# Local attention on one core: each pair's scores as two 64-row matmuls over three score banks, the value projection in the queries' bank, the output product one pair earlier, the queries' square behind ScalarE's copies

## The reference, cut to what matters

```
# per batch and layer: n = 2048 tokens, 8 heads of 64, windows of 128 tokens
q, k, v = split(shift_token(x) @ wqkv)             # 256 -> 3 x 512
q = l2norm(q) * q_scale;  k = l2norm(k) * k_scale
q, k = rotary_xpos(q, k)
# each window of 128 queries looks at its own 128 keys and the 128 before them
sim  = einsum('bhwid,bhwjd->bhwij', 8 * q, k2)     # 128 x 256 for a head and window
attn = softmax(where(mask, -big, sim))
x = x + einsum('bhwij,bhwjd->bhwid', attn, v2) @ wo
```

## Time and profile before

| | |
|---|---|
| median of 3 runs | 4049.13 us (4045.39 to 4050.89) |
| profiled execution | 4053.28 us, its span 4051.5 us |
| PE busy | 3685.3 us, 91% of the span |
| PEld, DVE, ACT, POOL busy | 44%, 69%, 51%, 22% |
| the four local attention stages, first transpose to last add | 1193.0 to 1479.2, 1619.0 to 1903.3, 3197.2 to 3483.1, 3622.6 to 3908.1 |

### The profile page before, as it was taken

How to read it: one execution, slowest core, us unless ns; L and a number is a source line. 1 busy time by engine, 2 the same in 40 slices (tenths; PEclk the granted TensorE clock), 3 DMA queues, 4 the chain that set the end, 5 groups by cost and what they waited for, 6 DMA issues and landing times. The chain is left out here.

```text
span 4051.5 us, 59853 instructions
## 1 busy us (share of the span) xinstructions
PE 3685.3 (91%) x19604; PEld 1769.1 (44%) x19604; DVE 2796.6 (69%) x7007; ACT 2072.7 (51%) x3717; POOL 895.6 (22%) x801
## 2 busy tenths in 40 slices
PE   7999977999979989998979999689999799899988
PEld 5333334333335555555543333343333455555555
DVE  2998866998856643665349987769987666436644
ACT  3366643466656641565125667334667566316641
POOL 2001015001024322332220010150010333213322
PEclk8899988899989999999989999889999899999999
DMA  4222002222020010100032220022220200110000
GB/s 94 38 33 33 1 3 52 36 33 33 1 66 6 1 54 6 28 1 6 21 75 33 33 33 2 2 56 32 33 33 1 66 6 1 54 28 6 1 11 26
DMA packets 129571, 109.04 MB, mean 27 GB/s; under 512 B 40884, under 2 KB 122332, under 8 KB 128220
## 3 DMA queue, kind: packets, MB, share of 16 engines
q1 hardware_dynamic: 129256, 105.12, 12.9%
HBM read 41.15 MB, written 4.19 MB: 11 GB/s over the span
## 5 line engine op out<-in xcount | busy, mean ns | idle before, releaser
L737 ACT ACTIVATE probs<-banks 128x1024 f32<-128x1024 f32 (+3 forms) x1280 | 1084.3, 894 | 677.6 <-PE banks L705 673.5
L776 DVE TENSOR_REDUCE chunk_max<-banks 128x1 f32<-128x512 f32 (+2 forms) x1728 | 1100.3, 684 | 113.3 <-PE banks L663 90.6
L663 PE MATMUL banks<-stack_k,stack_q 96*128 96x512 bf16 (+3 forms) x2560 | 791.0, 363 | 40.1 <-DVE chunk_max L776 21.1
L705 PE MATMUL banks<-stack_q,stack_k 99*128 99x512 bf16 (+3 forms) x2560 | 644.4, 351 | 6.8 <-ACT probs L737 3.0
L682 PE MATMUL banks<-probs,values 128*17 128x512 f32 (+3 forms) x5120 | 595.0, 537 | 8.1 <-ACT probs L737 5.3
L663 PEld LDWEIGHTS banks<-stack_k,stack_q 96*128 96x128 bf16 x2560 | 238.0, 99 | 693.8 <-DVE chunk_max L776 408.7
L630 POOL TENSOR_SCALAR_AFFINE_SELECT probs<-probs 128x512 f32<-128x512 f32 x256 | 164.2, 641 | 1658.6 <-ACT probs L737 1657.5
L1336 ACT ACTIVATE probs_l<-probs_l,nmax 128x256 f32<-128x256 f32 x512 | 255.9, 500 | 342.7 <-DVE nmax L1459 341.2
L1213 PE MATMUL banks<-wqkv,hT 128*128 128x512 f32 x768 | 357.4, 603 | 2.6 <-issue 2.6
L771 DVE CUSTOM_DVE_ANT_0 masked_scores<-banks,wide_mask 128x384 f32<-128x384 f32 (+1 forms) x512 | 304.4, 619 | 53.3 <-PE banks L663 49.1
L705 PEld LDWEIGHTS banks<-stack_q,stack_k 99*128 99x128 bf16 x2560 | 237.7, 99 | 233.2 <-ACT probs L737 39.8
(11 more groups left out here) (190 smaller groups left out, 4790.1 us busy)
## 6 DMA issues: line engine op xcount, KB each, us to landing
stack_q<-parts SPq DMA_DIRECT2D x384, 64.0 KB, 2.4
stack_k<-parts SPq DMA_DIRECT2D x384, 64.0 KB, 2.4
xpos<-in_c_xpos SPq DMA_DIRECT2D x4, 2048.0 KB, 8.0
wqkv<-in_L_ffn_wqkv SPq DMA_DIRECT2D x12, 512.0 KB, 14.0
w<-in_L_ffn_w SPq DMA_DIRECT2D x16, 320.0 KB, 3.3
x_tok<-in_L_attn_x SPq DMA_DIRECT2D x8, 512.0 KB, 5.8
rope<-in_c_rope SPq DMA_DIRECT2D x2, 2048.0 KB, 8.7
hs_f<-x_mid SPq DMA_DIRECT2D x16, 256.0 KB
```

The costliest lines, as they stand in the source:

```text
L663: ins = pe.matmul(out, sq[0:KS, c, j0 + j, i * P:(i + 1) * P], sk[0:KS, cc, j0 + j, 0:width], start=True, stop=not (diag and heads > 1), s ...
L705: ins = pe.matmul(ps[:, SCORE + j, off:CH], keys, sq[0:KS + PARTS, c, j, off:CH], start=True, stop=True, skip_group_check=True)
L737: act.activation(probs[:, s % 2, 2 * half:2 * half + 2, off:CH], ps[:, SCORE + 2 * half:SCORE + 2 * half + 2, off:CH], ACT.Exp)\
L776: dve.tensor_reduce(chunk_max[:, n % 2, j:j + heads, i, cc], bank[:, 0:heads * width].rearrange("p (h n) -> p h n", h=heads), AX.X, ALU.ma ...
```

## The change

- **Scores.** The keys are kept as `kT`, both heads' 64 rows on the partitions where the transposes put them, without zero blocks. `scores(n)` is two matmuls with 64 rows and 256 columns each: head 0 on partitions 0 to 63, head 1 on 64 to 127. Each half has a bank of its own out of three (3, 5, 6), and its own signal; half i waits for DVE's maximum over half i - 3.
- **The value projection** loses its bank and uses the queries' bank BQ, at p = 0 of its own window instead of p = 2 of the window before.
- **The order on PE.** p = 0: scores, v of this window, `turn_h(w+2)`, k of the next. p = 1: q of the next. p = 2: `out(w-1)`. p = 3: `turn_qk(w+1)`. Before: `turn_h`, k and q at p = 0, v at p = 2, `turn_qk` and `out` at p = 3.
- **ScalarE.** One copy of 128 partitions of keys for two of 64. `v_take(w)` behind `h_out` at p = 0. The square of the queries goes from p = 0 to p = 1, behind `p_out` and `o_out`.
- **DVE.** `maximum` waits and signals per half. The queries' rotation is in one piece behind `scale(4w+1)`; before, its first product stood between the maximum and the scale. `add(w-1)` goes from p = 3 to p = 2.

```diff
-    BH, BQ, BK, BV, BO, BS, BT = 0, 1, 2, 3, 4, 5, 7
+    BH, BQ, BK, BO, BT = 0, 1, 2, 4, 7
+    BS = (3, 5, 6)
-    PROJECTED = ((1, 0), (), (2,), ())
-        kbd = sb("k_blocks", [P, NP, 2, SLOT, P])
+        kT = sb("kT", [P, NP, SLOT, P])
 def project(w, i):
-                    bank, free, done = ((BQ, ("q_T_out", w), "qk_q"), (BK, ("k_T_out", 2 * w), "qk_k"),
-                                        (BV, ("v_out", w), "v_mm"))[i]
+                    bank, free, done = ((BQ, ("v_out", w), "qk_q"), (BK, ("k_T_out", w), "qk_k"),
+                                        (BQ, ("q_T_out", w + 1), "v_mm"))[i]
 def scores(n):
-                    if n >= 2:
-                        pe.wait_ge(S["maxed"], n - 1)
-                    pe.matmul(ps[:, BS + n % 2, :].rearrange("p (a b n) -> p a b n", a=2, b=2), qT[:, p, :],
-                              kbd[:, p, :, s0:s1 + 1:s1 - s0, :], start=True, stop=True, skip_group_check=True)\
-                        .then_inc(S["scored"], 1)
+                    for h in range(2):
+                        i = 2 * n + h
+                        rows = slice(h * LD, (h + 1) * LD)
+                        if i >= 3:
+                            pe.wait_ge(S["maxed"], i - 2)
+                        pe.matmul(ps[:, BS[i % 3], 0:2 * P].rearrange("p (b n) -> p b n", b=2), qT[rows, p, :],
+                                  kT[rows, p, s0:s1 + 1:s1 - s0, :], start=True, stop=True, skip_group_check=True)\
+                            .then_inc(S["scored"], 1)
 # PE, the loop over n
                         scores(n)
+                        if p == 0:
+                            project(w, 2)
                         if p == 0 and w + 2 < NT:
                             turn_h(w + 2)
-                        if w + 1 < NT:
-                            for i in PROJECTED[p]:
-                                project(w + 1, i)
-                        if p == 3:
-                            if w + 1 < NT:
-                                turn_qk(w + 1)
-                            if w:
-                                out(w - 1)
+                        if p < 2 and w + 1 < NT:
+                            project(w + 1, 1 - p)
+                        if p == 2 and w:
+                            out(w - 1)
+                        if p == 3 and w + 1 < NT:
+                            turn_qk(w + 1)
 # ScalarE, the loop over n
                         if p == 0 and w + 2 < NT:
                             h_out(w + 2)
-                        if w + 1 < NT:
-                            for i in PROJECTED[p]:
-                                if i < 2:
-                                    square(w + 1, i)
-                                else:
-                                    v_take(w + 1)
+                        if p == 0:
+                            v_take(w)
+                        if p == 0 and w + 1 < NT:
+                            square(w + 1, 1)
                     if n:
                         p_out(n - 1)
                     if p == 1 and w:
                         o_out(w - 1)
+                    if p == 1 and n < PAIRS and w + 1 < NT:
+                        square(w + 1, 0)
 # DVE, the loop over n
                     maximum(n)
-                    if p == 1 and ahead:
-                        rotate(w + 1, 0, (0,))
...
                     if p == 1 and ahead:
-                        rotate(w + 1, 0, (1,))
+                        rotate(w + 1, 0)
                         normalise(w + 1)
-                    if p == 3 and w:
+                    if p == 2 and w:
                         add(w - 1)
```

More of the change, by code:

```diff
@@ L1228, in scores @@
                         pe.wait_ge(S["q_T_out"], w + 1)
-                        pe.wait_ge(S["k_T_out"], 2 * (w + 1))
-                    if n >= 2:
-                        pe.wait_ge(S["maxed"], n - 1)
+                        pe.wait_ge(S["k_T_out"], w + 1)
                     s0, s1 = order(w)
-                    pe.matmul(ps[:, BS + n % 2, :].rearrange("p (a b n) -> p a b n", a=2, b=2), qT[:, p, :],
-                              kbd[:, p, :, s0:s1 + 1:s1 - s0, :], start=True, stop=True, skip_group_check=True)\
-                        .then_inc(S["scored"], 1)
+                    for h in range(2):
[6 more added lines that the diff above has]
+                            .then_inc(S["scored"], 1)
                 def turn_p(n):
@@ L1272, in _ @@
                 turn_h(0)
-                for i, come in ((1, "w_k"), (0, "w_q"), (2, "w_v")):
+                for i, come in ((1, "w_k"), (0, "w_q")):
                     pe.wait_ge(early[come], 16)
@@ L1282, in _ @@
                         scores(n)
+                        if n == 0:
+                            pe.wait_ge(early["w_v"], 16)
+                        if p == 0:
+                            project(w, 2)
                         if p == 0 and w + 2 < NT:
                             turn_h(w + 2)
-                        if w + 1 < NT:
-                            for i in PROJECTED[p]:
-                                project(w + 1, i)
-                        if p == 3:
-                            if w + 1 < NT:
-                                turn_qk(w + 1)
-                            if w:
-                                out(w - 1)
+                        if p < 2 and w + 1 < NT:
[4 more added lines that the diff above has]
+                            turn_qk(w + 1)
                     if 1 <= n <= PAIRS:
@@ L1319, in v_take @@
                     act.wait_ge(S["v_mm"], w + 1)
-                    act.copy(v[:, w % SLOT, :], ps[:, BV, :]).then_inc(S["v_out"], 1)
+                    act.copy(v[:, w % SLOT, :], ps[:, BQ, :]).then_inc(S["v_out"], 1)
                 def qk_out(w):
@@ L1325, in qk_out @@
                     act.wait_ge(S["k_T"], w + 1)
[L1326 to L1331, removed]
+                    act.copy(kT[:, :, w % SLOT, :], ps[:, BK, :].rearrange("p (n m) -> p n m", n=NP)).then_inc(S["k_T_out"], 1)
                 def exp(n):
-                    act.wait_ge(S["maxed"], n + 1)
+                    act.wait_ge(S["maxed"], 2 * (n + 1))
                     for h in range(2):
@@ L1350, in _ @@
                 square(0, 0)
-                v_take(0)
                 h_out(1)
@@ L1377, in _ @@
                 pool.memset(mhalf[:, :], -0.5).then_inc(S["halves"], 1)
-                pool.memset(kbd[:, :, :, :, :], 0.0).then_inc(S["zero_k"], 1)
+                pool.memset(kT[:, :, SLOT - 1, :], 0.0).then_inc(S["zero_k"], 1)
                 pool.memset(v[:, SLOT - 1, :], 0.0).then_inc(S["zero_k"], 1)
@@ L1398, in _ @@
                     if w >= 2:
-                        pool.wait_ge(S["maxed"], NP * (w - 1))
+                        pool.wait_ge(S["maxed"], 2 * NP * (w - 1))
                     pool.tensor_tensor(inv_q[:, w % 2, :], ssum[:, q], mhalf[:, q], ALU.pow).then_inc(S["inv_n"], 1)
@@ L1455, in maximum @@
                     m = later[:, 0 if w == 0 else 1 if w % SLOT == 0 else 2, :]
-                    dve.wait_ge(S["scored"], n + 1)
                     dve.wait_ge(S["p_T"], n + 1)
                     for h in range(2):
-                        ins = dve.tensor_tensor_reduce(out=pr[:, n % 2, h, :], in0=ps[:, BS + n % 2, h * 2 * P:(h + 1) * 2 * P],
-                                                       in1=m, scale=inv_q[:, w % 2, 2 * p + h:2 * p + h + 1], scalar=3e38, op0=ALU.add, op1=ALU.min,
-                                                       accum_out=nmax[:, n % 2, h:h + 1])
-                    ins.then_inc(S["maxed"], 1)
+                        dve.wait_ge(S["scored"], 2 * n + h + 1)
+                        dve.tensor_tensor_reduce(out=pr[:, n % 2, h, :], in0=ps[:, BS[(2 * n + h) % 3], 0:2 * P], in1=m,
+                                                 scale=inv_q[:, w % 2, 2 * p + h:2 * p + h + 1], scalar=3e38,
+                                                 op0=ALU.add, op1=ALU.min, accum_out=nmax[:, n % 2, h:h + 1])\
+                            .then_inc(S["maxed"], 1)
                 def scale(n):
```

## The result

The changed kernel takes 4070.82 us (median of 5 runs, 4068.39 to 4071.89) where the kernel before takes 4049.13 (4045.39 to 4053.55): ratio 1.005, 95% interval 1.0039 to 1.0061, slower by 21.7 us. The forecast was 4054, +5; direction and range held, the size did not. The profiled execution took 4070.75 and has a span of 4068.9.

What follows compares the result with a forecast made beforehand. PE bounds the kernel before; afterwards a DVE and ScalarE loop of 16.8 us a window. Per stage 1.2 - 2.4 + 2.0 = +0.8, four stages +3, median 4052 to 4053, some 2 for waits: 4054 us, range 4036 to 4082.

Steps and rivals of the forecast that it cites:

- What bounds the window: Steady window: PE sets the length before; afterwards the loop through DVE and ScalarE does, 16.8 us against PE's 15.4.
- the seven steps: Steady window's loop followed through PE, ScalarE and DVE in the new order: 16.8 us, 0.2 less than 17.00.
- The sign: Whole kernel: forecast slower, 4054 us; chances faster 0.14, same 0.39, slower 0.47.
- The score slot: PE, per score pair: halves side by side 0.63, then 0.11 open weights; 0.74 against 0.96, 0.22 less.
- Halves in series: Rival, PE's score pair: the two halves run one after the other, slot 0.43 longer, +24 us, 4078; chance 0.26.
- Three banks too few: Rival, score banks: half 1 comes too late for its slot every window, 0.4 each, +22 us, 4076; chance 0.09.
- PE stays the bound: Rival, steady window: loop shorter than 16.8 because squares come earlier; 3960 at its end, 4010 half way; chance 0.08.
- No price for the change of shape: Rival, PE around 64-row scores: switching tile shape is free, 0.2 less on the loop, -11 us, 4042; chance 0.09.
- Steps 1 and 2: Steady window: PE from pair 2's scale through the keys' projection, 5.5 us, then ScalarE's square of the keys, 0.83.
- The stage's ends: First and last windows of each stage: +1.2 us at the start, window 14 at 16.6, +2.0 for the last two.
- the v projection behind them then runs at half clock for some 0.55: First window, PE: term of 0.55 us for the value projection behind the half-clock first scores, within the start's +1.2.
- The sum: Whole kernel: +0.8 us a stage, four stages +3, median 4052 to 4053, some 2 for waits, forecast 4054.

Runs made afterwards that it cites:

- e5: Changed kernel with two of the four matmuls of each output product left out: 4060.5 us, one run.
- e3: Changed kernel with the queries' square directly behind exp of p = 1, ahead of ScalarE's two copies: 4043.12 us, ratio 0.9982 to the kernel before.
- e7: Changed kernel with idle transposes (24, 3 and 8) in PE's holes at each stage's start: 4048.11 us, ratio 1.0 to the kernel before.
- e6: Changed kernel with one of the two matmuls of each value projection left out: 4056.43 us, one run.
- e10: Kernel before the change with idle transposes (24, 3 and 8) in the first window's holes, nothing else: 4042.93 us, ratio 0.9982.
- e8: Changed kernel with the last window's old output order, the early queries' square and the idle transposes at the stage's start together: 4024.79 us, ratio 0.9934.
- e1: Changed kernel with output product and add back at p = 3 in the last window alone: 4054.24 us, ratio 1.0012 to the kernel before.
- e2: Changed kernel, order kept, with idle transposes (12, 5 and 6) in PE's holes at each stage's end: 4061.08 us, ratio 1.0029 to the kernel before.
- e9: As e8, but scores in one piece, with zero-padded key blocks, two key copies and two score banks: 4075.32 us, ratio 1.0061 to the kernel before.
- e12: As e8, but the key copy alone in two pieces of 64 partitions: 4046.73 us, ratio 0.9994 to the kernel before.

## Why the prediction was right and wrong

**What bounds the window: right.** PE's work fell and the window didn't follow; the loop of DVE and ScalarE took its place, at 16.76 where the seven steps gave 16.8. e5 took PE work away without shortening the window, e3 shortened the loop by moving one square. That the kernel came out slower is no merit of this: by layout alone a stage is 1.0 - 2.87 + 0.47 + 1.25 = -0.15, forecast +0.8, and neither can be told from no change. The sign was luck, and the clock brought it.

**The score slot: right.** 0.63 and then 0.10 of open weights were forecast as 0.63 and 0.11. *Halves in series* would have been 1.06 and is refuted by the row of 3328.86. *Three banks too few* shows once a stage, in window 0 (the 0.64 at 3234.00, 0.63 in e7), and in no steady window of the changed kernel. The room is small: with less PE work before pair 3 it shows in every window of e5. *PE stays the bound* fell with the two holes. *No price for the change of shape* fell with the 0.63.

**The loop: its length right, its path half right.** Steps 1 and 2 gave one way to the square of the keys, through PE's projections. e6 shows a second one beside it through ScalarE's own queue, of equal length. A reader of my steps would have expected 0.8 a window from less PE work and got 0.04.

**The stage's ends: the step that failed.** The forecast was +1.2 for the head and +2.0 for windows 14 and 15, and it measured +4.75 and +3.66. The layout itself was right: with the filled head it is +1.0 to +1.2 (e7 against e10), and windows 14 and 15 are +0.47 and +1.25. What failed is the clock in the sum of the ends. It has one term, "the v projection behind them then runs at half clock for some 0.55"; that projection took 3.08 instead of 1.82 (3220.66 to 3223.74), 1.26. For a new fall of the clock there is no term, neither in window 0 nor in window 15. I took the half-clock stretches as where they had been before, and let only the work move under them. The new order makes longer holes on PE at both ends: 1.69 and 0.64 in window 0, where the kernel before has none over 0.8 behind its first scores, and 1.90 in window 15. A further stretch at 1.2 GHz follows in window 0 and, where the clock fell, in window 15. Net of what the kernel before lost in the same way, that is 3.7 us a stage at the head and 1.9 at the tail, together as much as the four stages' 22.2; what they lost by layout, the steady windows gave back.

**The sum.** The forecast's +3 for the stages was +22.2. The 4.8 that the profiled execution gained outside them is in no term and is mostly the choice of execution; as e8 shows such differences come and go between kernels that are alike there.

## What to carry to other kernels

When PE stops being the bound, cost the holes that the new order leaves on it twice: as time, and as the clock that its next instructions will have. Here the steady windows have holes of 0.53 and 0.56 and the clock held in them; look at the first and the last turn, where an order made for the steady state leaves PE waiting. There either keep the old order (e1) or give PE idle work (e7); both were worth more here (16.6 and 22.7 us, of the latter 5 to 8 in the kernel before as well) than the change had gained in its steady windows (11.5). And when an experiment takes work off one path of a loop and nothing happens, look for a second path of the same length before calling the first wrong.

## What the runs showed of the hardware

- Two matmuls of 64 rows on the two row halves, each with a wait, a bank and a signal of its own, share their slot: four passes of 256 columns in 0.63, where `scores` in one piece holds its slot for 0.96.
- With idle transposes between PE's other work the granted clock stayed at 1.00 (e2's tail in four stages of four, windows 0 and 1 of e7). The Trainium skill (TensorE: Matmul & The Clock Gate, Part 4: PE-mode transpose) says that the full clock does not engage for transposes, which do not count as busy in the same way. As fillers they did keep the clock up here, and the measurement decides; whether transposes alone would raise it, no run here shows.
- PE's clock fell behind holes of at most 1.9 us with work between them (3488.31 to 3491.45), while the steady windows, with holes of 0.53 and 0.56, stayed at 1.00 throughout, and in six stages of 20 the same tail did too (e7, 1467.56 to 1472.22). The size of a hole alone does not tell: in stage 4 of e7 the clock is still 1.00 behind one of 2.76. Where the one turns into the other no run here says.

```profile
3624.39 0.63 PE L1222 MATMUL banks<-identf,prod_cos 128*128 128x128 f32 x4 [2.76 <-POOL prod_cos L1404]
```

- Two copies of 64 partitions took ScalarE 1.17 to 1.18, one of 128 partitions with the same 512 columns 0.59 (the rows of e8, e9 and e12).
